# Four stacked graph layers on one core: layer 0's softmax and sums in two halves, 24 blocks merged at the end, the index sort first in the plan

## The reference, cut to what matters

```
x = _layernorm(x + L0(x, edge_attr, src, dst, W1, W2, attn, bias))
x = _layernorm(x + L1(x, src, dst, edge_weight, ...))      # attention, an MLP, two norms
x = _layernorm(x + L2(x, src, dst, W, b))                  # degree-normalised sums by src
x = _layernorm(x + L3(x, src, dst, edge_weight))           # weighted sums by src

# L0
f      = concat(x[src], edge_attr) @ W1.T
logits = leaky_relu(concat(f, x[dst])) @ attn
alpha  = exp(logits - segment_max(logits, dst)[dst]) / segment_sum(exp(...), dst)[dst]
h      = segment_sum((x @ W2.T)[src] * alpha, dst) + bias
```

## Time and profile before

| what | value |
|---|---|
| median of 3 runs | 2683.65 us (2670.19 to 2685.36) |
| the profiled execution | 2680.65 us, span 2678.8 us |
| busy in the span | PE 67%, DVE 64%, POOL 63%, ACT 55% |
| first gather of u1, u2, u3 | 16.72, 281.12, 753.37 us |
| first scatter of u4, first gather of u5, u6 | 1215.79, 1522.48, 1827.62 us |
| first and last scatter of final | 2097.70, 2649.43 us |

### The profile page before, as it was taken

The page is one execution under the profiler, slowest core; times in us unless marked ns, Lnnn a source line. Parts: engine busy times, 40 slices in busy tenths (PEclk is TensorE's granted clock), DMA queues, the critical chain, the costliest instruction groups (busy, mean ns, idle before and its releaser), DMA issues. The chain is left out here.

```text
span 2678.8 us, 24741 instructions
## 1 busy us (share of the span) xinstructions
PE 1807.6 (67%) x7450; PEld 868.5 (32%) x7450; DVE 1724.8 (64%) x3305; ACT 1465.7 (55%) x2212; POOL 1679.7 (63%) x1610
## 2 busy tenths in 40 slices
PE   5999989767977888898999876568877654000000
PEld 3444444324533333344444324433322343000000
DVE  5888989988888787765555469887666775000002
ACT  3787777753676667677777755357777521000000
POOL 5777777710057771006777578775777787777774
PEclk9999999987997888899999986679999755555555
DMA  3333222214622221124444644432121233000002
GB/s 68 73 75 80 68 72 64 63 31 126 192 77 49 60 55 32 47 77 113 138 129 135 179 150 124 117 78 65 58 58 54 86 106 110 16 18 21 22 21 99
DMA packets 236808, 214.81 MB, mean 80 GB/s; under 512 B 157822, under 2 KB 170965, under 8 KB 236677
## 3 DMA queue, kind: packets, MB, share of 16 engines
q1 hardware_dynamic: 182228, 166.60, 21.7%
q0 software_dynamic: 51200, 46.31, 7.2%
q10 hardware_dynamic: 3248, 0.34, 0.1%
HBM read 140.36 MB, written 86.31 MB: 85 GB/s over the span
## 5 line engine op out<-in xcount | busy, mean ns | idle before, releaser
L2405 POOL DMA_INDIRECT stab<-wk,rank_i x200 | 215.0, 1075 | 267.4 <-DVE wk L621 209.1
L578 ACT ACTIVATE b_s<-ps,vec 128x512 f32<-128x512 f32 (+1 forms) x356 | 240.8, 682 | 137.7 <-PE ps L572 45.0
L2402 POOL DMA_INDIRECT e_bc<-x0tab,dpos_i x136 | 137.7, 1013 | 245.7 <-DMA x0tab<-e_bc 200.6
L2402 POOL DMA_INDIRECT u<-x2tab,dpos_i x200 | 227.8, 1139 | 80.2 <-issue 75.3
L809 DVE TENSOR_SCALAR b_x<-b_s 128x8 f32<-128x8 f32 x2 | 0.3, 167 | 396.4 <-DMA b_gl<-out_dram 396.4
L2402 POOL DMA_INDIRECT u<-x3tab,src_i x200 | 206.1, 1030 | 78.8 <-issue 59.4
L2402 POOL DMA_INDIRECT u<-in_x_dram,src_i x200 | 201.7, 1009 | 76.7 <-issue 56.9
L2402 POOL DMA_INDIRECT u<-in_x_dram,dst_i x200 | 207.7, 1038 | 64.3 <-issue 60.9
L2405 POOL DMA_INDIRECT out_dram<-u,sfin_i x200 | 196.5, 982 | 66.3 <-issue 66.3
L2405 POOL DMA_INDIRECT out_dram<-u,dst_i x176 | 197.2, 1120 | 60.6 <-issue 56.0
L566 PE MATMUL ps<-b_h,blk_c 128*128 128x512 f32 (+1 forms) x296 | 169.3, 655 | 35.6 <-ACT b_gl L586 35.1
(11 more groups left out here) (423 smaller groups left out, 4747.4 us busy)
## 6 DMA issues: line engine op xcount, KB each, us to landing
b_gl<-in_x_dram SPq DMA_DIRECT2D x98, 256.0 KB, 2.8
wk<-dlist SPq DMA_DIRECT2D x50, 500.0 KB
wk<-slist SPq DMA_DIRECT2D x50, 500.0 KB
out_dram<-b_gl SPq DMA_DIRECT2D x93, 256.0 KB, 2.0
u<-stab SPq DMA_DIRECT2D x25, 510.0 KB
x2none<-b_gl SPq DMA_DIRECT2D x25, 250.0 KB
x0tab<-e_bc SPq DMA_DIRECT2D x25, 240.0 KB
wk<-x2none SPq DMA_DIRECT2D x25, 240.0 KB
```

Source lines behind the costliest of these rows:

```text
L578: return nc.scalar.activation(b_s[l][:, 0:w], pB[l][:, 0:w], ACT.Abs_reciprocal_sqrt, bias=col(EPSV))
L2402: pool.indirect_dma_start(out=o, out_offset=None, in_=tab, in_offset=at_ix(ix), **kw).then_inc(s, 16)
L2405: pool.indirect_dma_start(out=tab, out_offset=at_ix(ix), in_=a, in_offset=None, bounds_check=last, oob_is_err=False).then_inc(s, 16)
```

## The change

**Two halves.** Layer 0's softmax is made in two phases, the first for the columns 0 to 99 and the second for the columns 100 to 199, and so are the ends (`JOBS`). `SPLIT` is 12. The first softmax needs the `l0` of all groups but the `l0d` of groups 0 to 12 alone. Then follow the ends of groups 0 to 12 in four chunks and the sums of groups 0 to 11. The second softmax needs the rest of `l0d`, takes up the running maximum and the running sum of the first (`kept`, `resumed`) and makes a factor by which the carried partial sum of the first half is scaled (`factor`, `carried_v`). Its ends take groups 12 to 24 in four chunks; the first copy of them waits for the first 12 sums (`agg_rows`), its scan for their stores. Then follow the sums of groups 12 to 24.

**The run over the border.** The sums of the target whose edges lie in both halves are right in the second half alone. `fixrow` copies that row of xd to all partitions (PE and DVE), and `fix 0..12` puts it into the first half's columns by `copy_predicated`, before `xd1` of the same group. Both have rank 2. From group 13 on, `l0d` uses the tile `w_e` as scratch and waits on DVE for the last `l0`.

**Ranks.** `ix` has rank 0 (1 before), `l0` and `l0d` have rank 1 (2 before), `prep2 0` rank 0 (1 before), DVE's plan begins at 24 us (44 before).

**Late blocks.** `LATE` is 24, so `final` waits for 74 blocks. The late blocks are loaded from `late_tab` into the part of `u` that the `only` scatters have read, after these; the loads of what the scatters left go in chunks of three with at most two chunks open; the merge is two operations (a mask, a `copy_predicated`) in place of three; the stores go out on ACT's queue, no longer on SP's.

```diff
-    LATE = 11
+    LATE = 24
+        PHASES = ((0, (0,)), (0, (1,)), (1, (0, 1)))
+        JOBS = ((0, (0,)), (0, (1,)), (1, (0, 1)), (2, (0, 1)), (3, (0, 1)))
+        SPLIT = QB // GC
-        unit(("ix", 0), 1, ...
+        unit(("ix", 0), 0, ...
-            unit(("l0", g), 2, ...
+            unit(("l0", g), 1, ...
+        half = [range(SPLIT + 1), range(SPLIT + 1, NG)]
+        unit(("sm", 0), 0, SM[0], [(("l0", g), "out", 0) for g in GROUPS] + [(("l0d", g), "b", 0) for g in half[0]] +
+             [(("ix", 0), f"s{index_at['derive']}", 0)])
+        unit(("sm", 1), 0, SM[1], [(("sm", 0), "wc", 0)] + [(("l0d", g), "b", 0) for g in half[1]])
+        ends_unit(1, [(("sm", 1), "wc", 0)], p0=[(("main", SPLIT - 1), "rows", 0)], scan=[(("main", SPLIT - 1), "out", STORED)])
-                 [(("lay", 0), "copy", CARRIED if g == 0 else 0), ...
+                 [(("lay", int(g >= SPLIT)), "copy", CARRIED if g in (0, SPLIT) else 0), ...
+        unit(("fixrow", 0), 2, "p pe .5 +e0;c dve .6 -e0", [(("main", SPLIT), "add", 0), (("sm", 1), "wc", 0)])
+        for g in range(SPLIT + 1):
+            unit(("fix", g), 2, "t dve .7", ...
-        unit(("prep2", 0), 1, PREP2, [(("lay", 0), "copy", 4.0), ...
+        unit(("prep2", 0), 0, PREP2, [(("lay", 1), "copy", 4.0), ...
-        START = dict(pe=44.0, act=44.0, dve=44.0, ...
+        START = dict(pe=44.0, act=44.0, dve=24.0, ...
+            sp.wait_ge(S("only_st"), 128 * NG)
-            sp.wait_ge(S("final_st"), 256 * NG)
+            sp.wait_ge(S("final_st"), 128 * NG)
             for k, j in enumerate(LATE_LOADS):
+                if k % FOUND == 0 and k >= 2 * FOUND:
+                    sp.wait_ge(*late_found(k - 2 * FOUND))
+        def late_act(act, t):
+            for k, j in enumerate(LATE_STORES):
+                act.wait_ge(S("late_step"), 2 * k + 2)
+                act.dma_start(late_rows(j), t3(late_o[j])).then_inc(S("late_dma"), 16)
-                nc.vector.tensor_scalar(m, o[:, :, 0], UNSET / 2, UNSET, ALU.is_lt, ALU.mult)
-                nc.vector.tensor_tensor(d, d, bc(m, D), ALU.add)
-                nc.vector.tensor_tensor(o, o, d, ALU.min)
+                nc.vector.tensor_scalar(m, o[:, :, 0], UNSET / 2, None, ALU.is_ge)
+                nc.vector.copy_predicated(o, m.bitcast(i32).unsqueeze(2).broadcast_to((128, GC, D)), late_d[j])
+            if resumed:
+                own(nc.vector.tensor_tensor(sc_b[:, P - 1:P], carry_b[:, 0, 1:2], m1[:, P:P + 1], ALU.subtract))
+                own(nc.vector.tensor_scalar(sc_b[:, P - 1:P], sc_b[:, P - 1:P], -1000.0, None, ALU.max))
+        def fix_dve(dve, t, g):
+            c0, c1 = GC * g, min(GC * g + GC, QB)
+            dve.wait_ge(S("xd_sum"), g + 1)
+            fixed[g] = stepped(nc.vector.copy_predicated(a, fix_of[...], fix_row...))
```

More of the change, by code:

```diff
@@ L275, in gnn_resnorm_kernel @@
[L275 to L281, removed]
@@ L283, in gnn_resnorm_kernel, with hops @@
-        CHUNKS = range(-(-NG // 4))
-        def ends_unit(layer, after, **deps):
+            unit(("l0d", g), 1, "a dve .7;b dve 1.41", [(("u2", g), "t", LANDED)] + ([(("l0d", g - 1), "b", 0)] if g else []) +
+                 ([(("l0", NG - 1), "f", 0)] if g == SPLIT + 1 else []))
+        def hops(c0, c1):
+            return ";".join(f"hop{k} dve .35;hop{k}a pe .9 +e1;hop{k}s dve 1.1 -e1;hop{k}b pe .6 +e1;hop{k}c dve {c} -e1" +
+                            (";exp act .5;sum dve .9" if k == 0 else "") for k, c in ((0, c0), (1, c1)))
@@ new lines, in gnn_resnorm_kernel, with chunks_of @@
+        unit(("sm", 1), 0, SM[1], [(("sm", 0), "wc", 0)] + [(("l0d", g), "b", 0) for g in half[1]])
+        unit(("sm", 2), 0, SM[2], [(("src", g), "h", 0) for g in GROUPS] + [(("xd1", g), "dot", 0) for g in GROUPS])
+        def chunks_of(j):
+            first, last = {(0,): (0, SPLIT + 1), (1,): (SPLIT, NG), (0, 1): (0, NG)}[JOBS[j][1]]
+            return [range(g, min(g + 4, last)) for g in range(first, last, 4)]
+        CHUNKS_BEFORE = [sum(len(chunks_of(k)) for k in range(j)) for j in range(len(JOBS))]
@@ L286, in ends_unit @@
+        def ends_unit(j, after, **deps):
             text = []
-            for c in CHUNKS:
+            for c in range(len(chunks_of(j))):
                 b = f"e{c % 2}"
@@ L334, in gnn_resnorm_kernel @@
                       "j pe 1.13;r act .7;h dve .75;" + LAST_MLP + "out dve 1.45",
[L335 removed]
+                      [(("lay", 2), "copy", CARRIED if g == 0 else 0)] + [(("xd1", g), "mul", 0)],
                       **(dict(out=[(("u4", g - 2), "t", STORED)]) if g >= 2 else {}))
@@ L1551, in carry_sp @@
+            n = 2 * len(hs) * nw * D
+            nc.vector.tensor_copy(rows_[0:QB, 0:n], e1[0:QB, 0:n]).then_inc(S("e1_free"), 1)
+        def carry_sp(sp, t, j):
+            layer, hs = JOBS[j]
+            n = len(hs) * (2 if layer == 1 else 1) * D
             rows_ = carry_tiles(layer)[2]
@@ L2374, in _ @@
             sp_programs += [prep2_sp(sp, at["prep2", k], k) for k in range(2)]
-            sp_programs += [carry_sp(sp, at["lay", layer], layer) for layer in range(4)]
+            sp_programs += [carry_sp(sp, at["lay", j], j) for j in range(len(JOBS))]
             sp_programs += [edges_sp(sp, n, dlist if n < 2 * NG else slist, t0) for n, t0 in EDGES]
@@ L2378, in _ @@
             sp_programs += [rload_sp(sp, at["rl", g], g) for g in GROUPS]
-            sp_programs += [unset_sp(sp, at["u3", 0]["t"] + 20 * j, j) for j in range(LATE)]
+            sp_programs += [unset_sp(sp, at["u3", 0]["t"] + 12 * j, j) for j in range(LATE)]
             sp_programs += [late_sp(sp, 1e6)]
@@ L2477, in _ @@
                         rows, ix = rdst[:, b, :] if g >= STAGED else staged(g)[:, D * k:D * k + D], fidx_i
-                    scatter(out, last_node, ix[:, b:b + 1], rows, S("final_st"))
+                    scatter(out, last_node, ix[:, b:b + 1], rows, S("only_st" if kind == "only" else "final_st"))
         @block.tensor
```

400 lines of the change are left out of this document (245 added, 155 removed).

## The result

Over four runs each the changed kernel took 2616.51 us (2610.02 to 2625.86) and the kernel before 2678.86: a ratio of 0.9764, with a 95% interval from 0.974 to 0.9788. It is faster by 62 us, where I had forecast 32. The profiled execution took 2617.53 us, its span 2615.8; the one of before took 2680.65, so the two spans differ by 63.0 us, and that is the sum to be taken apart here.

What follows compares the result with a forecast made beforehand. POOL was taken as the bound, its indirect transfers one behind the other but for two waits of about 200 us. Against 2680.65 us, -55 + 5 + 5 + 13 = -32 gave 2649, as a median 2652; range 2609 to 2694.

Steps and rivals of the forecast that it cites:

- The first gap: POOL's wait before the first gather of `u3`, about 200 us: forecast 55 us shorter, `u3` starting at 698.
- DVE's work: From 425 us to the start of `u3`: 251 us of work at a share of 0.92, through at 698.
- the other count, the chain: Behind the last `u2` gather: `l0d`, second softmax, ends, scan, 13 sums and last store, done at 686.
- the rival in which DVE is the wall: First half's sums find no room on DVE, second ends wait; `u3` starts at 725, total 2679; chance 0.17.
- the bound: In `u2`: twelve sums beside the gathers put off its end by up to 18 us, to 571.
- the fixes in the second gap: Before the first `u4` scatter: 13 `fix` operations on DVE, 9 us of work, add 5 us (0 to 10).
- the displaced dense work: Some 10 dense blocks move from the two gaps into stretches where POOL works: 5 us added (0 to 12).
- mid: Time from the first gather of `u3` to the first scatter of `final`; forecast 5 to 10 us longer.
- The dense work: Before `final`: 86 blocks through where 74 are needed, so no wait; a rival with `final` waiting gave 2716, chance 0.08.
- The end: From the last scatter to the end: DMA is the limit, 41 us, 13 more than before (+8 to +22).

Runs made afterwards that it cites:

- the second profile: The changed kernel run again with no edit: 2623.53 us, ratio 0.9794 to the kernel before.
- One edit without meaning: Planner constant `GRACE` at 0.12 in place of 0.1, in the kernel before (2673.57 us, ratio 0.9959) and in the changed kernel (2641.58 us, ratio 0.9869).
- the second drawing: The changed kernel with planner constant `GRACE` at 0.12 in place of 0.1: 2641.58 us, ratio 0.9869 to the kernel before.

## Why the prediction was wrong

**The first gap was right in size, and that was luck in part.** -55 was forecast for it and -52.6 measured; -56.9 in the second profile. I let DVE's work decide, at a share of 0.92: 251 us of work, through at 698. DVE was busy for 241 us, a share of 0.87, but that is not the work I had counted: 30 us of it are dense operations and 7 the fixes, neither of them in the 251. The counted work comes to 235 us by the same mean times, since 76 of the sort's stages fell behind 425 us and not 100; in the trace, where operations in a row overlap by about 0.1 us, it keeps DVE busy for 211. (Nor does the working for the start of that count come out: 12.75 groups of 10.7 us behind the first gather at 281.12 are 417.5, not 425; but the `l0d` of group 12 did start at 424.9 in the changed kernel.)

What the timeline shows is the other count, the chain, which had 686. It came to 700.8: 6.4 us later at its head (the last `l0d` ends at 563.2, forecast 556.8), 28.3 for the second softmax (30), 12.6 of waiting for the first half's sums (none in the chain's count), 14.1 for the ends (13.4), 10.1 from the scan to the first matrix of equal targets (11.6), and 72.1 from there to the first gather (64 and 10), with `prep2` and the fixes in between. That wait is the mechanism of the rival in which DVE is the wall, at about half of its price. Whether a less busy DVE and PE would have let the sums of the second half pass faster stays open: where dense blocks were held back, `u3` started no earlier, but the clock had fallen.

The gathers beside the sums were hardly slowed: `u2` lasted 277 us in the changed kernel (both profiles) and 271.6 and 274.7 in those of before. Of the 18 us that I took as the bound 3 to 6 appeared, and the late part alone, with no sums there, has 276.7. The Trainium skill (SBUF — State Buffer, Who interferes with whom) states that a VectorE instruction with two SBUF inputs contends with a GpSimd instruction that reads SBUF. What I had forecast with that rule in full, a `u2` that ends at 571 and a `u3` that starts at 704, did not come: `u2` ended at 557.7.

**The step that failed is what I let stand behind the gap.** I added 5 us for the fixes in the second gap and 5 for the displaced dense work, and let `u3` to `u6` stand as they were. Measured: `mid` is 20.9 us shorter (26.1 in the second profile) where I had it 5 to 10 longer. Between a `mid` 10 us longer and one 20.9 shorter lie nearly the whole of the missing 31 us. The rest is the end (10.6 for 13) less 2.4 in the gap. The fixes are not in the second gap at all: 10 of the 13 were planned between the sums, and seem to cost some us in the first gap; the last 3 run beside the first gathers of `u3`. Nor did POOL run transfer on transfer everywhere else, as I had it: in the trace of before it waits 18.0 us ahead of `u5` and 15.2 ahead of `u6`, which the change left at 17.5 and 13.2.

What the runs show in its place: a rank is an input to a planner that draws the order of all that follows, and another order has another second gap. One edit without meaning moved `mid` by -13.8 us in the kernel before and by +24.7 in the changed one, while the same program repeats it to 5 us. With the second drawing the whole gain is 33 us (2641.58 against 2674.38 on the same chip), about what I had forecast; beside the kernel before with the same edit it would be 0.9869 / 0.9959 = 0.991, some 24 us (an estimate from the two ratios).

So some 42 us (53 less 11) are what the halves, the ranks and the late blocks together do in the first gap and at the end, and the other 21 lie in stages that a redraw moves by as much. Of these, the 7.3 us of the second gap are of the kind that a drawing gives or takes. The 9.2 us of `u4` and `u5` are open: the late part alone took 10 to 13 us from these two stages with the order unchanged, and no run says why. Whether the ranks have an effect of their own behind `u3` (by their profiles they took 33 us from `mid` by themselves, the sort's rank 28) is not settled: it is of the size of a redraw.

**The dense work: the count was wrong, the conclusion held.** I expected 86 blocks through before `final`; 82 had passed DVE and 79 were stored. With 74 needed there is no wait, as forecast. With `LATE` at 11, where 87 are needed, my count would have had `final` wait for a few blocks at most, 10.6 us each; it waited 108.3 us and the kernel took 74 us more than the changed one. I had booked `LATE` as a cost paid at the end; it is what makes the change a gain. The blocks that gave way did so into `final`, beside the scatters: 16 of them where my count had left 12. What they cost there is no more than executions differ by (`final` 552.6 us, 560.8 in the second profile; 552.7 and 553.4 before).

**The end** was right: DMA busy to 0.88, 39.0 us where I had said 41. The predicated copy costs 0.73 us (L845), about what L811 did.

## What to carry to other kernels

- Where a planner writes the order, price a change of its inputs with a spread for every later stage, taken from a redraw that means nothing. Here such redraws moved the stages behind the change by -14 and +25 us. Run one before a gain or a loss of that size is given a cause, and a second profile of the same order beside it: some stages differ without any redraw.
- A gap between two phases is closed by its chain; work that gives way there must have another place. Count whether that place exists before the next deadline: here it was the last phase, and only the higher number of late blocks opened it.
- Parts of a change that are worth nothing alone can be worth much together: the ranks took 1 us from the gap, the halves added 18, both together took 57.

## What the runs showed of the hardware

When dense work was pushed out of the gathers of `u2`, the granted TensorE clock between 425 and 558 us was 0.52, close to its lower level of 1.2 GHz, with PE busy for 57 of 133 us; in the kernel before it was 0.97 there, close to the upper level of 2.4 GHz, with PE busy for 105 of 128. The same groups of the sums' matmuls took 422 and 439 ns each between 488 and 558 us in the changed kernel:

```profile
488.00:558.00 70.00, 31.76 (x192) 26.54 (x192) 64.15 (x131) 4.70 (x8) 54.19 (x52) 0.50 0.39 110
...
L1085 PE MATMUL ps<-wt,e_a 128*125 128x128 f32 x64 | 16.5, 439 | 9.1 <-DVE e_bc L1194 5.0 <-ACT e_a L1095 4.1
L1065 PE MATMUL ps<-wk 127*64 127x125 f32 x128 | 15.5, 422 | 38.6 <-DVE wk L1050 38.6
```

Against 276 ns at the granted clock of 1.00 this is (16 x 0.146) + (8 x 0.163) = 3.6 us more matmul time per sum, in the eight sums of this stretch, which are among the twelve for which the second ends then wait. How much of it lengthened that wait is not shown: PE itself waited 38.6 of these 70 us for DVE's L1050, and DVE was busy for 64 of them. The dense work on PE that looks like a burden was what went with the higher clock; the run with the dense blocks held in the first gap, where it was taken away by itself, shows that it kept the clock up for the second half.
